# Scores of the three attentions in two alternating sets of two PSUM banks, written a slot ahead in two ordered pairs of row groups

## The reference, cut to what matters

```python
x = x + L0_xattn(layernorm(x), ctx, ctx, mask, bias, ...)   # stage a0: queries, keys, values projected, bias and padding mask
x = x + L0_ffn(layernorm(x), ...)                           # stage f
x = x + L1_xattn(layernorm(x), ctx, ctx)                    # two matmuls with a gelu, in stage f
x = x + L1_ffn(layernorm(x), ...)                           # stage e1: 8 experts, top 2
x = x + L2_xattn(layernorm(x), ctx, ctx, W, b, mask)        # stage a2: no projections of q, k, v; causal mask
x = x + L2_ffn(layernorm(x), ...)                           # stages s2, e2: shared expert, 8 experts, top 1
x = x + L3_xattn(layernorm(x), ctx, ctx, Wq, Wk, Wv, Wo)    # stage a3: scores equal to 0 are masked
x = x + L3_ffn(layernorm(x), ...)                           # stage q3: int8 matmul

scores = einsum('bhqd,bhkd->bhqk', q, k) / sqrt(16) + bias or mask
out    = einsum('bhqk,bhkd->bhqd', softmax(scores), v) @ Wo
```

## Time and profile before

| what | value |
| --- | --- |
| median of 3 runs | 1098.03 us (1096.59 to 1098.26) |
| the profiled execution | 1100.99 us, its span in the trace 1099.2 us |
| mean granted TensorE clock | 0.89 of full speed |
| busy: PE, PE weight loads, DVE | 911.5, 623.4, 556.6 us |
| busy: ACT, POOL | 444.9, 392.7 us |
| stage a0, first to last scores | from 44.2 to some 148 us |
| stage a2 | from some 493 to 629 us |
| stage a3 | from 912.8 to some 1051 us |

### The profile page before, as it was taken

How to read it: one execution, slowest core, us unless ns; L and a number is a source line. 1 busy time by engine, 2 the same in 40 slices (tenths; PEclk the granted TensorE clock), 3 DMA queues, 4 the chain that set the end, 5 groups by cost and what they waited for, 6 DMA issues and landing times. The chain is left out here.

```text
span 1099.2 us, 18929 instructions
## 1 busy us (share of the span) xinstructions
PE 911.5 (83%) x5718; PEld 623.4 (57%) x5719; DVE 556.6 (51%) x1282; ACT 444.9 (40%) x874; POOL 392.7 (36%) x726
## 2 busy tenths in 40 slices
PE   6688887888699999935888889997999997888773
PEld 4466655776566666723555556653666674555441
DVE  4688865674722222227988735220211235767854
ACT  4355555552132222214555542221222225656634
POOL 5566642364400000036766512110000035766630
PEclk9799999996599999975878999998999996988965
DMA  5599510011211111127310030002111121110002
GB/s 182 156 365 385 183 48 1 20 49 39 101 57 58 61 58 61 53 75 275 136 32 18 2 130 30 23 30 72 38 48 48 39 43 23 16 16 11 2 1 77
DMA packets 74397, 84.17 MB, mean 77 GB/s; under 512 B 8299, under 2 KB 66643, under 8 KB 74323
## 3 DMA queue, kind: packets, MB, share of 16 engines
q1 hardware_dynamic: 68179, 70.65, 19.1%
q0 software_dynamic: 6144, 12.59, 4.2%
HBM read 45.73 MB, written 37.49 MB: 76 GB/s over the span
## 5 line engine op out<-in xcount | busy, mean ns | idle before, releaser
L1808 PE MATMUL PS<-WE,tmp 128*128 x496 | 186.9, 521 | 0.0
L1388 DVE TENSOR_TENSOR tmp<-PS,tmp 128x352 f32<-128x352 f32 (+1 forms) x78 | 47.4, 608 | 255.5 <-ACT tmp L918 255.5
L589 POOL TENSOR_TENSOR tmp<-tmp,small 128x616 f32<-128x616 f32 x96 | 116.7, 1216 | 92.7 <-DVE small L1053 92.5
L918 ACT ACTIVATE tmp<-PS 128x352 f32<-128x352 f32 (+1 forms) x78 | 41.4, 530 | 214.6 <-PE PS L1808 214.6
L1808 PEld LDWEIGHTS PS<-WE,tmp 128*128 128x128 f32 x496 | 91.8, 195 | 60.5 <-issue 36.1
L804 ACT ACTIVATE tmp<-PS 128x768 f32<-128x768 f32 x96 | 77.9, 811 | 104.9 <-PE PS L1584 104.2
L1830 PE MATMUL PS<-WE,tmp 128*128 (+1 forms) x418 | 101.0, 380 | 2.1 <-DVE tmp L1413 2.1
L1582 PE MATMUL PS<-ident,tmp 128*128 128x128 f32 x384 | 69.2, 309 | 34.6 <-POOL rsx L576 22.4
L1483 PE MATMUL PS<-ident,XN 128*128 128x128 f32 x208 | 40.4, 327 | 63.4 <-ACT XN L740 57.8
L740 ACT ACTIVATE XN<-X,SHIFTS,RSTDS 128x256 f32<-128x256 f32 x104 | 56.3, 590 | 71.9 <-POOL SHIFTS L531 71.8
L556 POOL DMA_INDIRECT WE<-ys,slot_u x16 | 15.8, 988 | 182.8 <-DMA ys<-tmp 179.7
(11 more groups left out here) (253 smaller groups left out, 1698.4 us busy)
## 6 DMA issues: line engine op xcount, KB each, us to landing
xs_regions<-WE SPq DMA_DIRECT2D x11, 1536.0 KB, 13.5
ys<-tmp SPq DMA_DIRECT2D x62, 128.0 KB, 1.7
WE<-in_L_w SPq DMA_DIRECT2D x16, 352.0 KB
tmp<-xs_regions SPq DMA_DIRECT2D x39, 128.0 KB, 2.0
WE<-in_L_rgT SPq DMA_DIRECT2D x8, 512.0 KB
WE<-in_L_ruT SPq DMA_DIRECT2D x8, 512.0 KB
WE<-in_L_rdT SPq DMA_DIRECT2D x8, 512.0 KB
tmp<-xs SPq DMA_DIRECT2D x23, 128.0 KB, 2.0
```

Source lines behind the costliest of these rows:

```text
L589: pool.tensor_tensor(sc, sc, spread(mx[:, q], SK), ALU.add).then_inc(shifted, 1)
L1808: last = pe.matmul(PS[:, 2 * q + k, 0:F], XS[:, q, c], w, start=c == 0, stop=c == G - 1)
```

## The change

A unit's scores go to two banks in place of four: chunks 0 and 1 side by side in one bank (columns 0 to 153 and 154 to 307), chunks 2 and 3 in the other. Even units use banks 0 and 1, odd units banks 2 and 3, so there are two sets. The readers on DVE and ACT read the same 616 numbers as 2 x 308. A bank now has two row groups that write it, so a unit's four chunks are no longer issued together: `half_scores(k, 0)` issues chunks 0 and 2, `half_scores(k, 1)` chunks 1 and 3, and the second waits for the new semaphore `half_psum`, which the first raises. PE writes unit s+1 in slot s: its first half where `scores(s)` stood, its second half behind `values` (in the first slots, which have no values, directly behind the first half). Unit 0 is written in slot 0 ahead of unit 1. The wait for `s_taken` is for the unit two before the one written.

```diff
@@
         FIRST_BANK, LEFT_BANK = 1, 3
         transposed = PS[:, BANK_PT:BANK_PT + 2].rearrange("p u n -> p (u n)")
         PT_PSUM = transposed[:, 0:PTW]
-        S_PSUM = PS[:, 0:CHUNKS, 0:PAIR]
+        TWO_SCORES = dict(a0=True, a2=True, a3=True)
+
+        HALVES = {stage: NU * sum(TWO_SCORES[early] for early in ("a0", "a2", "a3")[:i]) for i, stage in enumerate(("a0", "a2", "a3"))}
+
+        def s_psum_of(stage, k):
+
+            if TWO_SCORES[stage]:
+                return PS[:, 2 * (k % 2):2 * (k % 2) + 2, 0:2 * PAIR]
+            return PS[:, 0:CHUNKS, 0:PAIR]
+
 
 
@@
-        s_psum = sem("s_psum"); s_copied = sem("s_copied"); s_taken = sem("s_taken"); max_ready = sem("max_ready"); shifted = sem("shifted"); exp_done = sem("exp_done")
+        s_psum = sem("s_psum"); half_psum = sem("half_psum"); s_copied = sem("s_copied"); s_taken = sem("s_taken"); max_ready = sem("max_ready"); shifted = sem("shifted"); exp_done = sem("exp_done")
@@
 
                     act.wait_ge(s_psum, u0 + k + 1)
                     after(act, s_taken, u0 + k - 1)
-                    act.activation(Z[:, k % 2].rearrange("p (c n) -> p c n", c=CHUNKS), S_PSUM, ACT.Copy,
+                    scores = s_psum_of(stage, k)
+                    act.activation(Z[:, k % 2].rearrange("p (c n) -> p c n", c=scores.shape[1]), scores, ACT.Copy,
                                    scale=1.0 / FAR).then_inc(s_copied, 1)
 
                 for s in slots_of(stage):
@@
                     dve.wait_ge(s_psum, u0 + k + 1)
                     after(dve, pt_psum, u0 + k - 3 if k >= 4 else 0)
                     sc = SC[:, k % 4]
+                    scores = s_psum_of(stage, k)
+                    n = scores.shape[1]
                     if stage == "a3":
                         dve.wait_ge(s_copied, k + 1)
-                        dve.scalar_tensor_tensor(out=sc, in0=S_PSUM, scalar=0.0, in1=Z[:, k % 2], op0=ALU.is_equal,
+                        dve.scalar_tensor_tensor(out=sc, in0=scores, scalar=0.0, in1=Z[:, k % 2], op0=ALU.is_equal,
                                                  op1=ALU.subtract, reverse1=True).then_inc(s_taken, 1)
                     else:
-                        bias = BIAS[:, row].unsqueeze(1).unsqueeze(1).to_broadcast([P, CHUNKS, 2, SK])
-                        dve.tensor_tensor(sc.rearrange("p (c h k) -> p c h k", c=CHUNKS, k=SK),
-                                          S_PSUM.rearrange("p c (h k) -> p c h k", k=SK), bias, ALU.add).then_inc(s_taken, 1)
+                        bias = BIAS[:, row].unsqueeze(1).unsqueeze(1).to_broadcast([P, n, HG // n, SK])
+                        dve.tensor_tensor(sc.rearrange("p (c h k) -> p c h k", c=n, k=SK),
+                                          scores.rearrange("p c (h k) -> p c h k", k=SK), bias, ALU.add).then_inc(s_taken, 1)
                     dve.drain()
                     after(dve, shifted, u0 + k - 1 if k >= 2 else 0)
                     dve.tensor_reduce(mx[:, k % 2], sc.rearrange("p (h k) -> p h k", h=HG), AX.X,
@@
                         last = pe.matmul(PS[:, c, 0:PAIR], q, KBD[at, g, b], start=True, stop=True)
                     last.then_inc(s_psum, 1)
 
+                def half_scores(k, half):
+
+                    b, g, t = k // UNITS, k % UNITS // T, k % T
+                    if half == 0:
+                        if stage != "a2":
+                            pe.wait_ge(q_ready, q0 + b + 1)
+                        else:
+                            pe.wait_ge(xt_ready, norms + order["in", b] + 1)
+                        after(pe, s_taken, u0 + k - 1 if k >= 2 else 0)
+                    else:
+                        pe.wait_ge(half_psum, HALVES[stage] + k + 1)
+                    for c in (half, half + 2):
+                        at = slice(2 * DH * c, 2 * DH * (c + 1))
+                        q = XT[at, b, g, 1 + t * P:1 + (t + 1) * P] if stage == "a2" else QT[at, b % 2, g, t * P:(t + 1) * P]
+                        last = pe.matmul(PS[:, 2 * (k % 2) + c // 2, half * PAIR:(half + 1) * PAIR], q, KBD[at, g, b],
+                                         start=True, stop=True)
+                    last.then_inc(s_psum if half else half_psum, 1)
+
                 def transposes(k):
 
                     pe.wait_ge(rsx_ready, u0 + k + 1)
@@
                         queries(0)
                     if s == 0 and stage == "a3":
                         pe.wait_ge(blocks_ready, 12)
-                    if 0 <= s < NU:
+                    if TWO_SCORES[stage]:
+                        if s == 0:
+                            half_scores(0, 0)
+                            half_scores(0, 1)
+                        if 0 <= s < NU - 1:
+                            half_scores(s + 1, 0)
+                            if s < 3 + LATE[stage]:
+                                half_scores(s + 1, 1)
+                    elif 0 <= s < NU:
                         scores(s)
                     bl = batch_at(logits_slot, s)
                     if bl is not None and stage == "a2" and bl != B - 2:
@@
                         pe.wait_ge(blocks_ready, 4 * (layer + 1))
                     if 0 <= s - 3 - LATE[stage] < NU:
                         values(s - 3 - LATE[stage])
+                        if TWO_SCORES[stage] and s < NU - 1:
+                            half_scores(s + 1, 1)
                     bq = batch_at(queries_slot, s)
                     if bq is not None and bq > 0 and stage != "a2":
                         queries(bq)
```

## The result

| | before | changed |
| --- | --- | --- |
| median of the runs | 1097.31 us (1094.25 to 1098.26, 4 runs) | 1125.91 us (1117.36 to 1130.49, 4 runs) |
| ratio | | 1.0265, 95% interval 1.023 to 1.030 |
| profiled execution | 1100.99 us, span 1099.2 | 1123.37 us, span 1121.5 |
| granted clock over the span | 0.890 | 0.883 |

A forecast was written before the change was run, and what follows sets the result against it. No engine is full; chains between engines set the pace in three attentions. Terms +3.3 (a0), -2.1 (a2) and +6.9 (a3) sum to +8.1 us: 1109.1 profiled, 1106 forecast for the median, range 1093 to 1116.

The forecast's parts named there:

- The price of a pair: PE, every unit: two chunks take the 0.47 us that four took, so +0.47 a unit, +0.85 at half clock.
- a0: First attention: the pair between transposes and out-projection delays each of 7 batches by 0.47 us: +3.3 (-3.1 to +15).
- the 3.1 us of early waits: Start of a0: the few DVE waits for scores beyond the first 5.9 us, eaten by the first units' halves.
- a3: Attention where DVE waits for ACT's scaled copy: earlier scores don't help, added pairs count: +6.9 us (-2.2 to +15).
- 4.4 of the 6.9: In a3, second half delays the out-projection: three batches at half clock, 3 x 0.85, four at full, 4 x 0.47.
- a2: Attention where score waits go but values come later, gaining 0.3 us in each of 7 batches: -2.1 (-10.8 to +3.3).
- the sum of +8.1: Whole kernel: 3.3 - 2.1 + 6.9 us over the three attentions, taking the profiled execution from 1100.99 to 1109.1.
- The wait of 1.06 us: In a2, DVE's once-per-batch wait for scores, at 554.03, which was to go because the second half is ahead.
- 7 x 0.47: Upper bound for a2, +3.3 us: none of the waits gone and the values late.
- The clock rival: In a3 and a2, added PE work fills idle stretches, clock dips vanish: -1.4 us, 1097; chance 0.19.
- No cover: Each added pair lands on a chain at least half the time, or clock dips oftener: 1118 us; chance 0.10.
- The signs: Named as right: 0.45 to 0.5 us pairs, PE +30 us, a2 waiting for values, a0 batches near 14.2, longer a3 waits.

The follow-up runs named there:

- x_a0: The changed kernel's new scores in a0 only, old scores in a2 and a3: 1102.91 us, ratio 1.0074 to the kernel before.
- x_a3: The changed kernel's new scores in a3 only, old scores in a0 and a2: 1104.89 us, ratio 1.0082 to the kernel before.
- m_pairs: Kernel before plus 40 unused score matmuls on each of two row groups in slot 0 of a2: 1114.12 us beside 1100.14, one run.
- x_pairs: Kernel before with its four banks, one set and place, but chunks issued as two ordered pairs: 1123.99 us, ratio 1.026.
- x_first: Changed kernel without the second half of the scores from each stage's third unit on: 1102.83 us, ratio 1.0057 to the kernel before.
- x_adj: Changed kernel with each second half directly behind its first, ahead of the values: 1120.33 us, ratio 1.0204 to the kernel before.
- m_fours: Kernel before plus 160 unused score matmuls on all four row groups in slot 0 of a2: 1105.05 us beside 1100.14, one run.
- m_full: Kernel before plus 80 unused matmuls of all 128 rows in slot 0 of a2: 1106.58 us beside 1100.14, one run.

## Why the prediction was wrong

**The price of a pair was right.** 0.46 us at full clock, twice a unit, against the 0.47 taken, and 0.81 at half clock against 0.85.

**a0: right in the mechanism.** 14.16 us per batch where 14.18 (13.71 + 0.47) was forecast, and the DVE waits 6.9 us for the out-projection where it waited 3.6. The stage is +2.1 in the trace, and the first take another 2.0 later, of which 0.9 is its wait (6.8 us against 5.9). The first two batches came out 1.2 us shorter in sum and the third 1.0 longer, so of the 3.1 us of early waits next to nothing stayed. The runs of x_a0 say more, +8 with a lower bound of 4.5, and why is open.

**a3: near in size, not in mechanism.** +4.9 in the trace and +9 in the runs of x_a3, against +6.9. As forecast, no wait for the scaled copy went away. But 4.4 of the 6.9 were to come from a late out-projection, and the DVE's waits for it shrank, from 5.9 to 3.6 us (in x_a3 they are 7.1). By batches, the second is 4.1 us longer with 9.3 us at half clock in place of 1.2, the third and fourth are together 2.1 shorter with 3.4 in place of 13.6, and the last two and what follows them are 1.7 longer. That these come to a sum near the forecast's is in part luck.

**a2: the step that failed.** "So 0.3 of the 1.06 is left, 7 batches: -2.1 us", with +3.3 as its upper bound. It measured +11.6, and in the traced runs, where the sum of +8.1 came out at +22.4, this term is 13.7 of the 14.3 us missed. Two things in it were wrong. The wait of 1.06 us was taken from a stretch at half clock (550.4 to 553.8 in the clock record), as were eight of the nine waits for scores in a2 before, and is a product of it: with the old scores at full clock a batch already takes 16.65 us, so there was nothing to gain. And the pair was priced in a2 at full clock only, 0.47. At half clock it costs 0.8, PE is then nearly full (19.55 of 20.5 us), and a batch takes some 22 us, where before's took 17 to 19 with their shorter spells of half clock. A bound of "7 x 0.47" holds only if the clock is what it was.

**The clock rival had the wrong sign.** It said that added PE work would fill the idle stretches and hold the clock up. In the runs the granted clock went from 0.897 (mean of 19 runs of before and the profiled one) to 0.880 (4 runs). The runs of before alone, 1087.83 us at 0.911 to 1101.92 at 0.892, lie near a straight line of 5.8 us per 0.01; by it some 10 of the 29 us would go with the clock. This is an estimate: it goes beyond the clocks of these runs, and a batch with the new scores loses more at half clock than one with the old. The Trainium skill, in "TensorE: Matmul & The Clock Gate", HAM oscillation, puts the fall on gaps between bursts of matmuls. Here the clock fell at 592.8 with no idle time of PE over 0.50 us in the 10 us before, in the kernel before at 567.5 with none over 0.49, and it stayed down in 20.7 us without a gap (m_pairs): the measurement decides.

Do the pairs hold it down in the changed kernel? They alone cost as much as the whole change (x_pairs), and most of the loss goes when half of them go (x_first). Once the clock had come up in a2 and fell again, it was down for 3.4 to 13.7 us at a time in the three traces with the old scores there (before, x_a0, x_a3) and for 20.5 and 17.1 us in the changed kernel and in x_adj; x_pairs has 3.4, 13.7 and 20.5. That fits, but the pairs are not enough by themselves, as the second batch of x_pairs and x_adj shows. Why the clock falls at all, as at 592.8, was not settled; x_first has a low clock as well, without the second pair.

**"No cover" was the nearest**, at 1118 and a chance of 0.10. It was priced as half of the 45 us at full clock or a clock that dips oftener; it was both at once, a part on the chains and a part by the clock, and together they are 8 us more than it had.

**The signs said "right".** Pairs of 0.46 us, PE 48 us busier, 1.3 us of waits for scores in a2 with new ones of 6.4 for the values, batches of a0 of 14.16 us and 35.7 us of waits for the scaled copy in a3 all came as named; only the longer waits for the out-projection in a3 did not. None of the signs of being wrong came. They tested the price of a pair and a0, and none looked at the clock of a2, where the forecast failed.

## What to carry to other kernels

Matmuls on separate row groups cost the depth of one, so splitting four into two ordered pairs doubles their time on PE (0.46 us twice, where it was 0.48 once); a wait that this removes must be worth more than that, and must still be there at full clock. Before pricing a wait, look up the granted clock of its stretch: a wait at half clock may be an effect of it. When pricing added PE work, price it at both clocks, and do not count on busy row groups to bring the clock up: here those that filled half of the rows did not.

## What the runs showed of the hardware

The granted clock does not follow PE's busy time alone: 20.7 us of back-to-back matmuls on two of four row groups stayed at 1.2 GHz (m_pairs), while 12.9 us of the same on four row groups (m_fours), in the same place, and 23.2 us on all rows (m_full) brought it to 2.4 GHz. Nor does it need a long gap to fall: it fell at 592.8 in the changed kernel with PE idle for no more than 0.50 us at a time.

A loop that PE bounds at half clock is slow as long as the clock is down: a batch of a2 takes 16.7 us at full clock and some 22 at half, with PE busy 95% of it. That such a loop keeps itself at half clock is likely from m_pairs, but not shown.

A group of matmuls on two row groups takes PE as long as one on four: 0.46 us to the next tile shape against 0.48 at full clock.
